# Weight pieces of the other roles: one transfer over 128 partitions in place of four over 32, in a per-role adapter kernel

## The reference

```python
h = einsum('bsh,bhk->bsk', x, W_down[role]) + b_down[role]   # 1024 -> 512
h = gelu(h)                                                  # exact form
u = einsum('bsk,bkh->bsh', h, W_up[role]) + b_up[role]       # 512 -> 1024
y = x + u
yn = (y - mean(y)) * rsqrt(var(y) + 1e-5)
out = yn * gamma[role] + beta[role]
```

## Time and profile before

| | |
|---|---|
| median of 3 runs | 1424.94 us (1424.83 to 1425.28) |
| the profiled execution | 1425.9 us, its span 1424.0 us |
| TensorE (PE) busy | 1405.2 us, 99% |
| VectorE (DVE) busy | 1206.0 us, 85% |
| ScalarE (ACT) busy | 779.2 us, 55% |
| GpSimd (POOL) busy | 188.0 us, 13% |
| granted TensorE clock | 0.998 of full speed |
| DMA | 283.52 MB, of which GpSimd's queue 12.07 MB |

### The profile page before, as it was taken

One profiled execution on the slowest core, in us unless ns is written; L12 is line 12 of the kernel. 1 busy time (PEld: TensorE's weight loads), 2 busy tenths in 40 slices (PEclk: granted clock), 3 DMA queues, 4 the chain that ended last, 5 costly groups with the idle time before them and its releaser, 6 DMA issues.

```text
span 1424.0 us, 32330 instructions
## 1 busy us (share of the span) xinstructions
PE 1405.2 (99%) x6175; PEld 1158.7 (81%) x6176; DVE 1206.0 (85%) x1454; ACT 779.2 (55%) x2059; POOL 188.0 (13%) x297
## 2 busy tenths in 40 slices
PE   8999999999999999999999999999999999999997
PEld 6878888888888888888888888888888888888886
DVE  7789988788888888888888899888888888888888
ACT  5555555555555555555555555555555555555555
POOL 4367311100000000000000376311100000000000
PEclk9999999999999999999999999999999999999999
DMA  9678777866665665666566777777765666566563
GB/s 220 185 219 232 204 205 196 221 185 198 203 185 186 199 204 181 195 198 193 182 200 199 211 224 234 219 202 206 199 214 181 197 198 190 184 195 204 183 195 138
DMA packets 208726, 283.52 MB, mean 199 GB/s; under 512 B 25775, under 2 KB 155312, under 8 KB 208702
## 3 DMA queue, kind: packets, MB, share of 16 engines
q1 hardware_dynamic: 201726, 269.60, 61.6%
q0 software_dynamic: 5888, 12.07, 4.8%
q10 hardware_dynamic: 1088, 1.57, 0.4%
HBM read 183.27 MB, written 99.88 MB: 199 GB/s over the span
## 4 chain that ended last, share of the span: by engine, by line
PE 87%; DVE 6%; DVEq 4%; issue 3%; ACT 1%; DMA 0%; ACTq 0%; SPq 0%
PE p_down L989 14%; PE p_down L991 14%; PE p_down L990 14%; PE p_up L989 14%; PE p_up L991 14%; PE p_up L990 14%; DVEq L241 3%; DVE row L744 1%; DVE row L798 1%; DVE row L737 1%; DVE hT_lo L730 1%; DVE xT_raw L714 1%; DVE h L758 0%; DVE row L768 0%; DVE xT_lo L718 0%
## 5 line engine op out<-in xcount | busy, mean ns | idle before, releaser
L989 PE MATMUL p_up<-wu_hi,hT_hi 128*128 x1008 | 393.3, 390 | 2.9 <-DVE hT_lo L730 2.6
L989 PE MATMUL p_down<-wd_hi,xT_hi 128*128 x1012 | 394.3, 390 | 0.0
L990 PE MATMUL p_down<-wd_lo,xT_hi 128*128 x1012 | 393.9, 389 | 0.0
L991 PE MATMUL p_down<-wd_hi,xT_lo 128*128 x1012 | 393.7, 389 | 0.0
L991 PE MATMUL p_up<-wu_hi,hT_lo 128*128 x1008 | 392.2, 389 | 0.0
L990 PE MATMUL p_up<-wu_lo,hT_hi 128*128 x1008 | 392.2, 389 | 0.0
L559 ACT ACTIVATE hT_hi<-p_hT 128x512 fp32r<-128x512 f32 x126 | 75.5, 599 | 401.4 <-DVE p_hT L724 399.2
L744 DVE SCALAR_TENSOR_TENSOR row<-p_up,row 128x1024 f32<-128x1024 f32 x126 | 154.2, 1224 | 153.8 <-PE p_up L991 143.5
L545 ACT ACTIVATE xT_hi<-xT_raw 128x1024 fp32r<-128x1024 f32 x125 | 132.8, 1062 | 174.7 <-PE p_down L991 116.9
L989 PEld LDWEIGHTS p_up<-wu_hi,hT_hi 128*128 128x128 f32 x1008 | 188.9, 187 | 45.5 <-issue 6.6
L989 PEld LDWEIGHTS p_down<-wd_hi,xT_hi 128*128 128x128 f32 x1012 | 190.3, 188 | 40.7 <-issue 1.1
(11 more groups left out here) (164 smaller groups left out, 951.2 us busy)
## 6 DMA issues: line engine op xcount, KB each, us to landing
x_quad<-in_x SPq DMA_DIRECT2D x510, 128.0 KB, 3.5
row<-in_x SPq DMA_DIRECT2D x126, 512.0 KB, 4.0
out<-row SPq DMA_DIRECT2D x126, 512.0 KB, 2.8
h_dram<-h SPq DMA_DIRECT2D x125, 256.0 KB, 4.0
h_quad<-h_dram SPq DMA_DIRECT2D x500, 64.0 KB, 2.0
w_raw<-in_L_cond_W_down POOLq DMA_DIRECT2D x64, 64.0 KB, 3.6
w_raw<-in_L_cond_W_up POOLq DMA_DIRECT2D x64, 64.0 KB, 3.0
row<-in_L_cond_W_up SPq DMA_DIRECT2D x16, 128.0 KB, 5.3
```

Source lines behind the costliest of these rows:

```text
L989: pe.matmul(dst, a_hi, w_hi, start=first, stop=False)
L990: pe.matmul(dst, a_hi, w_lo, start=False, stop=False)
L991: return pe.matmul(dst, a_lo, w_hi, start=False, stop=last)
```

## The change

The two loops of GpSimd issue one DMA for each buffer in place of four. Two new views of the weights have the chunk as the outer dimension, and within it the quarter q, the row a and the column, so that one source pattern of 4 x 32 x 512 elements fills all 128 partitions. A buffer's semaphore rises by 16 for a filling in place of 64, and the counts that are waited for are scaled to that. What is computed, and the order of everything else, is as it was.

```diff
+        wd_chunk = W_down.rearrange("r (q c a) k -> r c q a k", q=NQ, a=BLK)
+        wu_chunk = W_up.rearrange("r (q c a) h -> r c q a h", q=NQ, a=BLK)
...
-                raw0 = (part - 1) * (DN // 2 + UN // 2) * 64
+                raw0 = (part - 1) * (DN // 2 + UN // 2) * 16
                 split0 = (part - 1) * (DN + UN)
                 with pool.Fori(0, DN // 2) as m:
                     for par in range(2):
-                        for q in range(NQ):
-                            src = wd_view[bass.ds(r, 1), q, :, bass.ds(2 * m + par, 1), :].rearrange("o a c k -> (o a) (c k)")
-                            pool.dma_start(w_raw[par][BLK * q:BLK * q + BLK, :], src).then_inc(pool_raw[par], 16)
+                        src = wd_chunk[bass.ds(r, 1), bass.ds(2 * m + par, 1)].rearrange("o p q a k -> (o p) q a k")
+                        pool.dma_start(w_raw[par][:, :], src).then_inc(pool_raw[par], 16)
                     for par in range(2):
-                        split_piece(par, raw0 + 64 * m + 64, split0 + 2 * m + par + 1, wd_hi, wd_lo,
+                        split_piece(par, raw0 + 16 * m + 16, split0 + 2 * m + par + 1, wd_hi, wd_lo,
                                     weights_at + 2 * PC * m + PC * par)
                     pool.wait_ge(pieces_split, split0 + 2 * m + 3)
-                raw0 += DN // 2 * 64
+                raw0 += DN // 2 * 16
...
-                        for q in range(NQ):
-                            src = wu_view[bass.ds(r, 1), q, :, bass.ds(m, 1), PC * par:PC * par + PC].rearrange(
-                                "o a c h -> (o a) (c h)")
-                            pool.dma_start(w_raw[par][BLK * q:BLK * q + BLK, :], src).then_inc(pool_raw[par], 16)
+                        src = wu_chunk[bass.ds(r, 1), bass.ds(m, 1), :, :, PC * par:PC * par + PC].rearrange(
+                            "o p q a h -> (o p) q a h")
+                        pool.dma_start(w_raw[par][:, :], src).then_inc(pool_raw[par], 16)
```

More of the change, by code:

```diff
@@ L487, in _ @@
                     for par in range(2):
-                        for q in range(NQ):
-                            src = wu_view[bass.ds(r, 1), q, :, bass.ds(m, 1), PC * par:PC * par + PC].rearrange(
-                                "o a c h -> (o a) (c h)")
-                            pool.dma_start(w_raw[par][BLK * q:BLK * q + BLK, :], src).then_inc(pool_raw[par], 16)
+                        src = wu_chunk[bass.ds(r, 1), bass.ds(m, 1), :, :, PC * par:PC * par + PC].rearrange(
+                            "o p q a h -> (o p) q a h")
+                        pool.dma_start(w_raw[par][:, :], src).then_inc(pool_raw[par], 16)
                     for par in range(2):
-                        split_piece(par, raw0 + 64 * m + 64, split0 + 2 * m + par + 1, wu_hi, wu_lo,
+                        split_piece(par, raw0 + 16 * m + 16, split0 + 2 * m + par + 1, wu_hi, wu_lo,
                                     weights_at + 2 * PC * m + PC * par)
```

## The result

The changed kernel takes 1445.76 us (median of 6 runs, 1441.10 to 1450.49), the kernel before 1425.11 (6 runs, 1421.46 to 1427.62). The ratio is 1.0147, 95% interval 1.0129 to 1.0166. The forecast was 1424.5, no difference, with a range of about 1421 to 1428. The time lies outside it.

What follows compares the result with a forecast made beforehand. TensorE, busy 99%, was taken as the bound, with 5.5 us lost in GpSimd's loops. First loop -1.9, second +1.5, sum -0.4 from 1425.9 gives 1425.5; less 1.0 for the timed runs, 1424.5, range about 1421 to 1428.

Steps and rivals of the forecast that it cites:

- The ground: TensorE busy 99%, GpSimd's loading hundreds of microseconds from any deadline; only disturbance in GpSimd's two loops, 5.5 us, can change.
- the beat: Start of the sum over p_up (L744), once per batch; 10.876 us each in the undisturbed stretch.
- the four operations with two SBUF inputs: VectorE's L798, L737, L718, L768: 1.2 to 1.3 us alone, up to 2.35 while GpSimd computes, not while it issues DMAs.
- the 5.5 us: Time lost in GpSimd's two piece loops, 5.0 in the first and 0.5 in the second; all the change can act on.
- the landing: One 256 KB load of w_raw in GpSimd's loops, from issue to arrival, taken as 4.0 us.
- The bounds I wrote, 2.0 and 6.1: Fastest and slowest 64 KB transfer of w_raw in us, taken as limits for a 256 KB load's arrival.
- The sentence on the Trainium skill: A DMA's engines follow its slowest dimension; the new source's 4 would make 4 of 16, though GpSimd's path makes exceptions.
- as walked: First loop: from the second on, groups of casts and subtractions fall on L737, L718, L768, clear of L798, 0.25 us each.
- The prediction's own sign of being wrong: Beat changed outside the loops, VectorE slowed by issues alone, SP's transfers arriving after over 8 us, or L798 slow in eight batches.
- the rival of few engines: 256 KB crowds a few DMA engines, SP's row of x arrives after 11.9 us, VectorE waits: 1445 us; chance 0.04.
- The rival "lands no sooner": The 256 KB transfer arrives no sooner than the four it replaces, 7 us; iterations 12.5 to 14, 1425 us; chance 0.21.
- GpSimd's issue time: Per loop iteration two issues of 0.54, 1.1 us (bounds 0.5 and 2.3), replace eight of 4.53; 3.4 saved off the path.

Runs made afterwards that it cites:

- The paced run: Kernel before with its four transfers, loaded two pieces ahead, GpSimd splitting one piece per batch between L798 and L737: 1421.03 us, ratio 0.9976.
- the store put first: Kernel before with SP's store of h issued ahead of its load of the row of x: 1420.64 us, ratio 0.9977.
- the runs with 4, 8 and 16 blocks: Changed kernel, each 256 KB source in 4 blocks of 32 rows as it stands (1445.76 us), 8 of 16 (1423.14) or 16 of 8 (1424.53).
- the run with equal distances: Changed kernel, each 256 KB transfer read from 128 DRAM rows of equal distance in place of four blocks: 1425.28 us, ratio 1.0008.

## Why the prediction was wrong

**The ground held.** Loading is far from its deadline; the beat outside the loops stayed 10.88; the four operations with two SBUF inputs are slowed by GpSimd's computing and not by its issues. The paced run took some 4 of the 5.5 us back, which supports the prediction's reading; the store put first took 3.6 back in another way, 2.7 of it in the loops, so it is not shown that the slowing alone cost them.

**The step that failed is the landing.** "I take 4.0, the row of 512 KB that SP loads" was 8.7 and 9.7. The bounds I wrote, 2.0 and 6.1, came from 64 KB transfers that, by the packet counts, give each engine one packet of 4096 B; a source of four blocks gives four engines 16 packets each. The sentence on the Trainium skill said just this (DMA: Bandwidth & Descriptors, "Why a DMA increments its semaphore by 16 and not by 1"), and the runs with 4, 8 and 16 blocks agree: 9, 5.4, 4.2 us. With the landing right, the rest of the forecast came out within the noise: that is the run with equal distances, 1425.3, its iterations of 11.0 us, the work on L718 and L768 as walked. The prediction's own sign of being wrong, a landing of SP's over 8 us, is what the trace shows.

**The second failure is the rival of few engines.** I gave it 0.04 and priced it at 1445, which is what came, but on the wrong wait, so the number agreed by luck. I tested one transfer, the row, whose landing (6.4 and 7.4 us on average in the two loops, at most 9.8) stayed under its beat. The store of h is in the same queue and had less room, 9.3 us from issue to use with a landing of 4.3. But that room alone doesn't give the price either: a landing of 9.5 is only 0.2 us more. What the walk left out is SP itself, which waits for the store to land before it goes on to the reload and the next store, 4.2 us of issuing later. "It needs three times today's landing" was said of the row; for SP's round one and a half times is enough, since it gets longer than the beat at a landing of 6.7 us. The rival "lands no sooner" had the landing about right (0.21, 7 us) and stopped there: it never asked whom a slow transfer slows.

**GpSimd's issue time.** Two issues took 1.37 us, not 1.1 (687 ns each with four blocks, 520 with sixteen); this cost nothing. POOL busy fell by 46 us, as said.

## What to carry to other kernels

Before merging transfers, write down how many engines the merged one uses, which is set by the outer dimension of its source as well as by the 128 partitions, and how many bytes that puts on each. A long transfer on a few engines slowed the transfers of another queue here, so price it there, not at its own reader. For each of them ask two things: how long after its landing it is used, and whether the engine that issues it waits for it before it issues the next. In the second case the landing is part of a round that has to fit into the beat. And where one wait is cured by reordering a queue, look for where the same time comes back before trusting it.

## What the runs showed that I had not expected

After TensorE had stood still for 3.08 us, until 140.94, it ran for about 1 us as before and then at half clock. The windows from 142.2 to 145.4 and from 146 to 153 of the changed kernel:

```profile
142.20:145.40 3.20, 3.20 (x9) 2.43 (x9) 3.11 (x5) 0.96 (x2) 0.00 (x0) 0.50 0.91 273
146.00:153.00 7.00, 7.00 (x32) 5.77 (x32) 3.86 (x5) 2.92 (x9) 2.96 (x3) 1.00 0.65 139
```

The granted clock was 0.50 (1.2 GHz) and then 1.00 (2.4 GHz) again, so, as an estimate, the stall cost some 1.6 us more than its length. In the ten batches from 798.78 the mean clock was 0.97.

And SP's store of h ahead of its row load makes the kernel before 0.23% faster, though VectorE never waited for that store. In the first loop the store then lands in under 4 us, against up to 6.3 before. Most of the gain, 2.7 us, is in the twenty batches of the loops shown above; by which wait it gets to TensorE was not found out.
